# SyncE's order of transfers in a hybrid attention stage: the write of the turned keys ahead of the reads of u, and ahead of the weight loads

## The chip, the core and the metric

The kernel runs on one core of one Trainium2 chip. The metric is the device time of one execution in microseconds (us); lower is better. A core has a matrix engine (TensorE, PE in the profile; its weight loads, PEld, overlap its matmuls), VectorE (DVE), ScalarE (ACT), GpSimd (POOL), and SyncE (SP), which in this kernel issues every DMA. Each engine runs its own list of instructions in order, and the engines wait for each other by semaphores.

## The reference

The input x is 2 x 2048 x 256 in fp32. Four residual layers follow one another; the change lies in the third.

```python
x = x + attn_a(layernorm(x))      # gated scan
x = x + ffn(layernorm(x))         # ternary weights, gelu
x = x + attn_b(layernorm(x))      # the stage of this study, "C" in the kernel
x = x + ffn(layernorm(x))

# attn_b, 16 heads of 64; q, k, v are projections of the layer's input
def step(carry, qkv):
    S_K, C_QV, G = carry
    q_t, k_t, v_t = qkv
    k_C = einsum('bhk,bhkv->bhv', k_t, C_QV)
    G = G + k_t[..., :, None] * k_C[..., None, :]
    S_K = S_K + k_t[..., :, None] * k_t[..., None, :]
    C_QV = C_QV + q_t[..., :, None] * v_t[..., None, :]
    S_C = einsum('bhkj,bhjv->bhkv', S_K, C_QV)
    o_t = einsum('bhk,bhkv->bhv', q_t, S_C - G)
```

## The kernel before

Stage C cuts the sequence into chunks of 128 tokens and works through 32 turns (`UNITS`). Turn j handles one chunk and half of the heads of both batches, in the form of masked score matrices plus a carried state. The order of every engine's work is written out by hand, one loop over j for each engine.

TensorE's list in turn j is: the scores of the queries with the keys (`scores_of`, L1027, into the banks SB), the product with the state (`by_state`, L1039), the second scores of turn j-1 with u as keys (L1027 again), `u_by_scores` of turn j (L1047), `state_change` and `o_by_scores` of turn j-1 (L1064, L1069, L1081), and then what `between(j)` puts there. That last part sets the kind of the turn:

- **projecting turns** (`qk_set(j)`: j % 4 is 3 or 0): the queries and keys of a coming half are projected (`project`, L201 to L203), with the output product of turn j-1 (L1096 to L1098) in the middle;
- **turns without projections**: the values of a coming chunk are projected (`values`, L1013 to L1015), and in one turn of eight (j % 8 is 5) the next block's normalised rows are transposed as well.

Two operands of TensorE are needed in rows instead of columns: the keys (`krow`) and u (`urow`). Both are turned in three steps. DVE transposes 32 x 32 blocks (`turn_keys` L1269 into `k32`, `turn_u` L1276 into the first half of `sc_a`). SyncE writes that tile to DRAM (the **save**, 512 KB, L914) and, once it has landed, reads it back in another order with four DMAs of 128 KB (the **lands**, L917): the keys back into `k32`, u into the second half of `sc_a`. ACT copies the landed tile into `krow` or `urow` (`store_rows`, L1200). TensorE waits for `krow` of turn j before `u_by_scores(j)` (`krow_done`), and for `urow` of turn j-1 before `state_change(j-1)` (`urow_done`).

Some order holds around these copies. ACT copies `urow` of turn j and then `krow` of turn j+1, after the last copy of a projection (the `urow` copy of a projecting turn stands before the last two of them). DVE masks the scores of turn j+1 into `sc_a` (`mask_scores`, L1258) only after `urow` of turn j was copied, since `sc_a` also holds the landed u; the second scores of TensorE need the banks that this mask empties. DVE turns u of turn j, adds two tiles of outputs (L1299), and then turns the keys of turn j+1; in a projecting turn these keys are projected in that very turn. SyncE also loads the projection's weights from DRAM into `ring_hi` and `ring_lo` (`load_weights`, L934; x = 1 are the keys' weights, x = 0 the queries'), four DMAs of 256 KB for each x, as TensorE is done with the weights that lie there.

Of the kernel before, what the change touches and what calls it, by code (L numbers as in the profile page):

```python
# [25 lines left out]
NSUB = T // SUB  # L26
GP = 4
UNITS = NSUB * 4
# [5 lines left out]
def hybrid_kernel(nc, x_d, gamma_d, wqkva_d, wq_d, wk_d, wv_d, wo_d, w1_d, b1_d, w2_d, b2_d, out_d):  # L34
# [13 lines left out]
    with outer:  # L48
        def sbuf(stack, name, shape, dtype=FP32):
            return stack.enter_context(nc.sbuf_tensor(name, shape, dtype))  # L50
# [58 lines left out]
        rows_dram = {x: nc.dram_tensor(f"{x}_rows_scratch", (P, 4, 8 * 32), FP32, kind="Internal").ap() for x in ("k", "u")}  # L109
# [734 lines left out]
        with ExitStack() as st:  # L844
# [7 lines left out]
            k32 = sbuf(st, "k32", [P, 4, 2, 4, 32])  # L852
# [3 lines left out]
            turned = sc_a[:, 0:2, :, :].rearrange("p a m t -> p (a m t)").rearrange("p (t g m d) -> p t g m d", t=4, g=2, m=4)  # L856
            landed = sc_a[:, 2:4, :, :].rearrange("p a m t -> p (a m t)").rearrange("p (r g m d) -> p r g m d", r=4, g=2, m=4)
# [12 lines left out]
            u_turned, u_saved, u_landed, urow_done = sem("C_uturned"), sem("C_usaved"), sem("C_uland"), sem("C_urow")  # L870
            k_turned, k_saved, k_landed, krow_done = sem("C_kturned"), sem("C_ksaved"), sem("C_kland"), sem("C_krow")
# [8 lines left out]
            LAST_STATE = UNITS - 2  # L880
# [10 lines left out]
            def qk_set(j):  # L891

                if j % 4 == 0:
                    return j // 2 + 1 if j < UNITS else None
                return (j + 1) // 2 if j % 4 == 3 and j + 1 < UNITS else None
# [10 lines left out]
            def ring_of(ring, x, pp, pairs=1):  # L906

                return ring[:, :].rearrange("p (n x c) -> p n x c", n=GP, x=2)[:, pp:pp + pairs, x, :]

            @block.sync  # L910
            def _(sp):
                def move(scratch, turned_tile, landed_tile, saved, landing, count):

                    sp.dma_start(scratch, turned_tile.rearrange("p t g m d -> p t (g m d)")).then_inc(saved, 16)  # L914
                    sp.wait_ge(saved, 16 * (count + 1))
                    for t in range(4):
                        sp.dma_start(landed_tile[t * 32:(t + 1) * 32, :, :, :, :].rearrange("p r g m d -> p r (g m d)"),  # L917
                                     scratch.rearrange("(r p) t c -> t p r c", r=4)[t]).then_inc(landing, 16)

                def move_k(j):  # L920
                    sp.wait_ge(k_turned, 2 * (j + 1))
                    move(rows_dram["k"], k32[:, :, :, :, :], k32[:, :, :, :, :], k_saved, k_landed, j)

                def move_u(j):
                    sp.wait_ge(u_turned, 2 * (j + 1))
                    move(rows_dram["u"], turned, landed, u_saved, u_landed, j)

                def load_weights(s, x):

                    for pp in range(0, GP, 2):  # L930
                        sp.wait_ge(qk_ready, 8 * (s - 1) + GP * (1 - x) + pp + 2)
                        pair = slice(s % 2 * GP + pp, s % 2 * GP + pp + 2)
                        for part, ring in ((0, ring_hi), (1, ring_lo)):
                            sp.dma_start(ring_of(ring, x, pp, 2).bitcast(FP32), wqk_dram[part][:, pair, x, :])\  # L934
                                .then_inc(slot_loaded[(1 - x) * 2 + pp // 2], 16)

                move_k(0)
                for x in (1, 0):
                    load_weights(1, x)
                for j in range(UNITS):  # L940
                    if j < LAST_STATE:
                        move_u(j)
                    s = qk_set(j)
                    if s is not None and s + 1 < 2 * NSUB:
                        load_weights(s + 1, 1)
                    if j + 1 < UNITS:
                        move_k(j + 1)
                    if s is not None and s + 1 < 2 * NSUB:
                        load_weights(s + 1, 0)
                    if j == UNITS - 3:  # L950
                        sp.wait_ge(v_ready, 4 * 2 * NSUB)
                        sp.dma_start(wv_hi[:, :, :].rearrange("p a b -> p (a b)").bitcast(FP32), w1t_dram).then_inc(tern_loaded, 16)
                        sp.dma_start(wv_lo[:, :, :].rearrange("p a b -> p (a b)").bitcast(FP32), w2t_dram).then_inc(tern_loaded, 16)
                for x in range(GP):
                    sp.wait_ge(slot_loaded[x], 32 * (2 * NSUB - 1))
                sp.wait_ge(tern_loaded, 32)
                sp.wait_ge(k_landed, 64 * UNITS)
                sp.wait_ge(u_landed, 64 * LAST_STATE)
# [392 lines left out]
```

## Time and profile before

| what | value |
|---|---|
| time, median of 3 runs | 1164.42 us (1162.98 to 1165.89) |
| time of the profiled execution | 1162.61 us |
| its span, first to last instruction | 1160.9 us |
| mean granted TensorE clock over the span | 0.983 of full speed |
| stage C in the trace | from about 280 us to 1025 us of the span |
| TensorE busy | 1090.5 us, 94% of the span |
| VectorE, ScalarE, GpSimd busy | 689.1, 573.8, 212.1 us |
| DMA | 124.20 MB, mean 107 GB/s |

Busy time of an engine that others do not wait for says little. What counts is the time in which TensorE stands idle, what ended that idleness, and the times at which the transfers behind it were issued. Times of rows are microseconds from the span's start. In a row of the timeline the first number is the start, the second how long the instruction or the merged group took, xN the number of instructions, and the bracket the idle time of the engine before it with what ended it.

### The profile page before, as it was taken

How to read it: one execution, taken by the hardware profiler on the slowest of the kernel's cores; microseconds unless marked ns; L12 is line 12 of the kernel's file. 1: busy time of each engine (PE TensorE's matmuls, PEld its weight loads, DVE VectorE, ACT ScalarE, POOL GpSimd, SP SyncE). 2: the span in 40 equal slices, each digit the busy share in tenths (PEclk: the TensorE clock that was granted, in tenths of full speed). 3: DMA queues.
4: the chain of work that ended last, by engine and by line, in shares of the span. 5: the costliest groups of instructions: out<-in, count | busy, mean ns of one | idle time of the engine just before them, and what ended most of it. 6: DMA issues, size and time to landing. Idle time of an engine off the chain costs nothing. (4 is left out here: it accounts for less than half of the span.)

```text
span 1160.9 us, 26806 instructions
## 1 busy us (share of the span) xinstructions
PE 1090.5 (94%) x11150; PEld 974.2 (84%) x11150; DVE 689.1 (59%) x1281; ACT 573.8 (49%) x1001; POOL 212.1 (18%) x177
## 2 busy tenths in 40 slices
PE   5897799998899999999999999999999999779998
PEld 4675588897789998898989899988889888768987
DVE  6999697771353574355475445466445357357783
ACT  4222666662454454445455544555455445246663
POOL 2326262120010101001110110021001010122230
PEclk9998899999999999999999999999999999899999
DMA  9000360003434524543642552453453344101011
GB/s 300 22 1 1 117 212 36 0 1 104 151 107 147 167 93 130 181 128 104 181 155 74 164 180 94 147 164 116 137 168 124 114 128 147 37 2 37 19 36 55
DMA packets 96320, 124.20 MB, mean 107 GB/s; under 512 B 8784, under 2 KB 86480, under 8 KB 95440
## 3 DMA queue, kind: packets, MB, share of 16 engines
q1 hardware_dynamic: 96208, 122.59, 33.0%
q8 instruction: 85, 1.39, 0.5%
q14 instruction: 27, 0.22, 0.1%
HBM read 79.57 MB, written 42.99 MB: 106 GB/s over the span
## 5 line engine op out<-in xcount | busy, mean ns | idle before, releaser
L972 POOL TENSOR_TENSOR ot_lo<-o_sum,ot_hi 128x512 fp32r<-128x512 f32 x64 | 82.3, 1289 | 644.6 <-ACT ot_hi L1194 642.4
L1258 DVE TENSOR_TENSOR sc_a<-bank,causal 128x512 f32<-128x512 f32 x128 | 79.6, 684 | 98.4 <-PE bank L1027 97.5
L1225 ACT COPY ut<-bank 64x512 f32<-64x512 f32 x128 | 74.2, 579 | 66.9 <-PE bank L1047 64.5
L201 PE MATMUL bank<-ln_xhi,ring_hi 128*128 128x512 f32 x256 | 102.4, 400 | 3.8 <-POOL state L962 3.3
L202 PE MATMUL bank<-ln_xlo,ring_hi 128*128 128x512 f32 x256 | 100.6, 393 | 0.0
L203 PE MATMUL bank<-ln_xhi,ring_lo 128*128 128x512 f32 x256 | 100.3, 392 | 0.0
L1258 DVE TENSOR_TENSOR ln_xn<-bank,causal 128x512 f32<-128x512 f32 x128 | 79.5, 684 | 34.3 <-PE bank L1027 34.3
L1200 ACT COPY krow<-k 128x512 f32<-128x512 f32 x64 | 36.4, 616 | 120.5 <-DMA k<-k_rows_scratch 120.5
L1269 DVE STREAM_TRANSPOSE k<-kt 128x512 f32<-128x512 f32 x64 | 43.4, 697 | 72.8 <-ACT kt L1184 72.8
L1320 DVE TENSOR_TENSOR xres<-bank,xres 128x512 f32<-128x512 f32 x32 | 22.0, 689 | 105.7 <-PE bank L1098 105.7
L1096 PE MATMUL bank<-wo_hi,ot_hi 128*128 128x256 f32 x256 | 74.9, 292 | 8.5 <-POOL ot_lo L972 8.5
L815 DVE TENSOR_TENSOR D_hid_lo<-D_hidden,D_hid_hi 128x512 fp32r<-128x512 f32 x64 | 57.5, 921 | 32.1 <-ACT D_hid_hi L764 31.6
L1291 DVE TENSOR_TENSOR state<-bank,state 128x512 f32<-128x512 f32 x60 | 41.5, 692 | 58.2 <-PE bank L1069 58.2
L1229 ACT COPY o_sum<-bank 64x512 f32<-64x512 f32 x128 | 74.2, 579 | 2.4
L1184 ACT COPY qt<-bank 128x512 f32<-128x512 f32 x64 | 37.4, 586 | 75.4 <-PE bank L203 75.4
L815 DVE TENSOR_TENSOR B_hid_lo<-B_hidden,B_hid_hi 128x512 fp32r<-128x512 f32 x64 | 59.6, 954 | 25.3 <-ACT B_hid_hi L764 24.9
L1097 PE MATMUL bank<-wo_lo,ot_hi 128*128 128x256 f32 x256 | 74.2, 290 | 0.0
L1098 PE MATMUL bank<-wo_hi,ot_lo 128*128 128x256 f32 x256 | 74.1, 289 | 0.0
L1047 PE MATMUL bank<-sc_a,krow 128*64 128x128 f32 x1024 | 63.5, 277 | 10.7 <-ACT krow L1200 10.5
L1047 PEld LDWEIGHTS bank<-sc_a,krow 128*64 128x64 f32 x1024 | 55.6, 137 | 15.6 <-ACT krow L1200 13.7
L775 ACT ACTIVATE D_hidden<-bank,b_sb 128x512 f32<-128x512 f32 x64 | 44.2, 692 | 47.7 <-PE bank L713 41.7
L1027 PEld LDWEIGHTS bank<-qt,kt 64*128 64x128 f32 x1024 | 59.7, 188 | 9.0 <-issue 5.3
(124 smaller groups left out, 2992.5 us busy)
## 6 DMA issues: line engine op xcount, KB each, us to landing
k_rows_scratch<-k SPq DMA_DIRECT2D x32, 512.0 KB, 4.0
k<-k_rows_scratch SPq DMA_DIRECT2D x128, 128.0 KB, 2.8
ring_hi<-wqk_hi_scratch SPq DMA_DIRECT2D x60, 256.0 KB, 3.9
ring_lo<-wqk_lo_scratch SPq DMA_DIRECT2D x60, 256.0 KB, 4.9
u_rows_scratch<-sc_a SPq DMA_DIRECT2D x30, 512.0 KB, 2.6
sc_a<-u_rows_scratch SPq DMA_DIRECT2D x120, 128.0 KB, 2.9
out_dram<-xres SPq DMA_DIRECT2D x6, 512.0 KB, 2.9
xres<-in_L_attn_a_x_dram SPq DMA_DIRECT2D x4, 512.0 KB, 7.3
```

The lines of the kernel that those rows point to most:

```text
L201: nc.tensor.matmul(out, w_hi, x_hi, start=(k == 0), stop=False)
L202: nc.tensor.matmul(out, w_hi, x_lo, start=False, stop=False)
L203: return nc.tensor.matmul(out, w_lo, x_hi, start=False, stop=(k == last_k))
L815: nc.vector.tensor_tensor(hid_lo[:, b, f, :], hidden[:, f % 4, :], hid_hi[:, b, f, :].bitcast(FP32), ALU.subtract).then_inc(hlow_done, 1)
L972: nc.gpsimd.tensor_tensor(ot_lo[:, g, :, :].rearrange("p m t -> p (m t)"), o_sum[:, (j - 1) % 2, g, :], ot_hi[:, g, :, :].rearrange("p m t ...
L1047: last = nc.tensor.matmul(bank[CB[2 * g + h]][half(h), m * P:(m + 1) * P], krow[:, j % 2, g, m, half(h)], sc_a[:, 2 * g + h, m, :], start= ...
L1096: nc.tensor.matmul(dst, ot_hi[:, g, m, :], w[0], start=first, stop=False)
L1097: nc.tensor.matmul(dst, ot_hi[:, g, m, :], w[1], start=False, stop=False)
L1098: last = nc.tensor.matmul(dst, ot_lo[:, g, m, :], w[0], start=False, stop=done)
L1225: nc.scalar.copy(ut[half(h), g, :, :].rearrange("p m t -> p (m t)"), bank[CB[x]][half(h), :])\
L1229: nc.scalar.copy(o_sum[half(1 - h), j % 2, g, :], bank[CB[x]][half(1 - h), :]).then_inc(os_done, 1)
L1258: nc.vector.tensor_tensor(to[:, x, :, :], bank[SB[x]][:, :].rearrange("p (m t) -> p m t", m=4), causal[:, None, :].to_broadcast([P, 4, P]) ...
```

## The change

The helper `move` (save, wait for it, four lands) is cut into `save_turned` and `land_rows`, and SyncE's loop gets another order. Nothing else changes: no instruction is added or removed, and the lists of the other engines stay as they are.

```diff
-                move_k(0)
+                save_k(0)
+                land_k(0)
                 for x in (1, 0):
                     load_weights(1, x)
                 for j in range(UNITS):
+                    s = qk_set(j)
                     if j < LAST_STATE:
-                        move_u(j)
-                    s = qk_set(j)
-                    if s is not None and s + 1 < 2 * NSUB:
-                        load_weights(s + 1, 1)
-                    if j + 1 < UNITS:
-                        move_k(j + 1)
-                    if s is not None and s + 1 < 2 * NSUB:
-                        load_weights(s + 1, 0)
+                        save_u(j)
+                    if s is not None:
+                        if j < LAST_STATE:
+                            land_u(j)
+                        save_k(j + 1)
+                        land_k(j + 1)
+                        if s + 1 < 2 * NSUB:
+                            load_weights(s + 1, 1)
+                            load_weights(s + 1, 0)
+                    else:
+                        if j + 1 < UNITS:
+                            save_k(j + 1)
+                        if j < LAST_STATE:
+                            land_u(j)
+                        if j + 1 < UNITS:
+                            land_k(j + 1)
```

```diff
+                def save_turned(scratch, tile, ready, saved, count):
+
+                    sp.wait_ge(ready, 2 * (count + 1))
+                    sp.dma_start(scratch, tile.rearrange("p t g m d -> p t (g m d)")).then_inc(saved, 16)
+
+                def land_rows(scratch, tile, saved, landing, count):
+
+                    sp.wait_ge(saved, 16 * (count + 1))
                     for t in range(4):
```

SyncE's list in a turn without projections (turn 5), before. C_uturned and C_kturned are the semaphores of DVE's transposes, C_usaved and C_ksaved those of the saves.

```order
L914 DMA u_rows_scratch<-sc_a 128x1024 [waits C_uturned]
L917 DMA sc_a<-u_rows_scratch 32x4x256 [waits C_usaved]
L917 DMA sc_a<-u_rows_scratch 32x4x256 x3
L914 DMA k_rows_scratch<-k 128x1024 [waits C_kturned]
L917 DMA k<-k_rows_scratch 32x4x256 [waits C_ksaved]
L917 DMA k<-k_rows_scratch 32x4x256 x3
```

The same turn in the changed kernel, whose line 915 is the save and 921 the lands:

```order
L915 DMA u_rows_scratch<-sc_a 128x1024 [waits C_uturned]
L915 DMA k_rows_scratch<-k 128x1024 [waits C_kturned]
L921 DMA sc_a<-u_rows_scratch 32x4x256 [waits C_usaved]
L921 DMA sc_a<-u_rows_scratch 32x4x256 x3
L921 DMA k<-k_rows_scratch 32x4x256 [waits C_ksaved]
L921 DMA k<-k_rows_scratch 32x4x256 x3
```

The keys' save has moved past the wait for u's save and the four reads of u, and those reads now stand behind the wait for the turned keys.

SyncE's list in a projecting turn (turn 3), before, behind that turn's u. C_qk counts the projected tiles of TensorE.

```order
L934 DMA ring_hi<-wqk_hi_scratch 128x2x256 [waits C_qk]
L934 DMA ring_lo<-wqk_lo_scratch 128x2x256
L934 DMA ring_hi<-wqk_hi_scratch 128x2x256 [waits C_qk]
L934 DMA ring_lo<-wqk_lo_scratch 128x2x256
L914 DMA k_rows_scratch<-k 128x1024 [waits C_kturned]
L917 DMA k<-k_rows_scratch 32x4x256 [waits C_ksaved]
L917 DMA k<-k_rows_scratch 32x4x256 x3
L934 DMA ring_hi<-wqk_hi_scratch 128x2x256 [waits C_qk]
L934 DMA ring_lo<-wqk_lo_scratch 128x2x256
L934 DMA ring_hi<-wqk_hi_scratch 128x2x256 [waits C_qk]
L934 DMA ring_lo<-wqk_lo_scratch 128x2x256
```

The same place in the changed kernel, whose line 942 is the weight load:

```order
L915 DMA k_rows_scratch<-k 128x1024 [waits C_kturned]
L921 DMA k<-k_rows_scratch 32x4x256 [waits C_ksaved]
L921 DMA k<-k_rows_scratch 32x4x256 x3
L942 DMA ring_hi<-wqk_hi_scratch 128x2x256 [waits C_qk]
L942 DMA ring_lo<-wqk_lo_scratch 128x2x256
L942 DMA ring_hi<-wqk_hi_scratch 128x2x256 [waits C_qk]
L942 DMA ring_lo<-wqk_lo_scratch 128x2x256
L942 DMA ring_hi<-wqk_hi_scratch 128x2x256 [waits C_qk]
L942 DMA ring_lo<-wqk_lo_scratch 128x2x256
L942 DMA ring_hi<-wqk_hi_scratch 128x2x256 [waits C_qk]
L942 DMA ring_lo<-wqk_lo_scratch 128x2x256
```

The four loads of the keys' weights have moved behind the whole move of the keys; the four of the queries' weights stand where they stood.

## Rows read from the trace of the kernel before

**Rows 1.** Busy time by stage: us, PE, PEld, DVE, ACT, POOL, PEclk, DMA share, GB/s

```profile
280.00:1002.00 722.00, 705.05 (x8861) 640.67 (x8861) 373.25 (x645) 358.30 (x638) 87.00 (x76) 1.00 0.43 138
```

**Rows 2.** Who waited for whom: us in total, times, longest us

```profile
ACT krow L1200 <- DMA k<-k_rows_scratch: 120.5, 30, 8.2
ACT urow L1200 <- DMA sc_a<-u_rows_scratch: 14.9, 12, 2.6
PE bank L1047 <- ACT krow L1200: 10.5, 12, 4.1
```

**Rows 3.** Timeline of PE at three of these waits

```profile
315.43 0.77 PE L1047 MATMUL bank<-sc_a,krow 128*64 128x128 f32 x10 [4.09 <-ACT krow L1200]
...
540.28 1.42 PE L1047 MATMUL bank<-sc_a,krow 128*64 128x128 f32 x22 [0.47 <-ACT krow L1200]
...
908.00 1.97 PE L1047 MATMUL bank<-sc_a,krow 128*64 128x128 f32 x32 [1.44 <-ACT krow L1200]
```

**Rows 4.** Busy time around the longest wait and around the one at 908

```profile
316.70:320.10 3.40, 3.40 (x60) 3.40 (x58) 0.40 (x1) 3.08 (x6) 0.00 (x0) 0.50 0.07 23
907.00:911.00 4.00, 3.00 (x74) 3.01 (x76) 1.24 (x3) 2.75 (x6) 0.00 (x0) 1.00 0.01 4
```

**Rows 5.** Timeline of SP, turn 10, without projections

```profile
525.94 0.34 SPq L914 DMA_DIRECT2D u_rows_scratch<-sc_a  x1
528.58 1.73 SPq L917 DMA_DIRECT2D sc_a<-u_rows_scratch  x4
530.36 0.43 SPq L914 DMA_DIRECT2D k_rows_scratch<-k  x1
533.87 1.73 SPq L917 DMA_DIRECT2D k<-k_rows_scratch  x4
```

**Rows 6.** Timeline of DVE, same stretch

```profile
527.01 1.28 DVE L1269 STREAM_TRANSPOSE k<-kt 128x512 f32<-128x512 f32 x2
...
535.37 2.48 DVE L1258 TENSOR_TENSOR sc_a<-bank,causal 128x512 f32<-128x512 f32 x4 [0.39 <-PE bank L1027]
```

**Rows 7.** Timeline of ACT, same stretch

```profile
532.79 1.14 ACT L1200 COPY urow<-sc_a 128x512 f32<-128x512 f32 x2 [0.78 <-DMA sc_a<-u_rows_scratch]
539.09 1.14 ACT L1200 COPY krow<-k 128x512 f32<-128x512 f32 x2 [5.16 <-DMA k<-k_rows_scratch]
```

**Rows 8.** Timeline of PE, same stretch

```profile
537.85 1.95 PE L1027 MATMUL bank<-qt,ut 64*128 64x128 f32 x32
```

**Rows 9.** Busy time and DMA, one microsecond of the same stretch

```profile
527.00:528.00 1.00, 1.00 (x6) 0.84 (x5) 1.00 (x3) 0.66 (x2) 0.00 (x0) 1.00 1.00 410
```

**Rows 10.** Timeline of SP, turn 7, a projecting one

```profile
462.51 0.34 SPq L914 DMA_DIRECT2D k_rows_scratch<-k  x1
469.94 1.74 SPq L917 DMA_DIRECT2D k<-k_rows_scratch  x4
...
473.24 0.47 SPq L934 DMA_DIRECT2D ring_lo<-wqk_lo_scratch  x1
```

**Rows 11.** Timeline of ACT, then PE, behind turn 7

```profile
474.23 1.14 ACT L1200 COPY krow<-k 128x512 f32<-128x512 f32 x2 [4.16 <-DMA k<-k_rows_scratch]
...
480.93 0.50 PE L201 MATMUL bank<-ln_xhi,ring_hi 128*128 128x512 f32 x1
```

**Rows 12.** Timeline of SP, turn 0, the first projecting one

```profile
298.82 3.05 SPq L917 DMA_DIRECT2D sc_a<-u_rows_scratch  x4
...
303.93 0.47 SPq L914 DMA_DIRECT2D k_rows_scratch<-k  x1
310.00 1.74 SPq L917 DMA_DIRECT2D k<-k_rows_scratch  x4
```

**Rows 13.** Timeline of DVE, then ACT, behind turn 0

```profile
300.40 0.71 DVE L1269 STREAM_TRANSPOSE k<-kt 128x512 f32<-128x512 f32 x1 [1.50 <-ACT kt L1184]
...
314.24 1.14 ACT L1200 COPY krow<-k 128x512 f32<-128x512 f32 x2 [7.69 <-DMA k<-k_rows_scratch]
```

**Rows 14.** The weight loads' line, from issue to landing, us

```profile
DMA to landing us min/median/max: 3.1/4.3/7.1
```

More of the change, by code:

```diff
@@ L911, in _, with save_k, land_k, save_u @@
             def _(sp):
-                def move(scratch, turned_tile, landed_tile, saved, landing, count):
-                    sp.dma_start(scratch, turned_tile.rearrange("p t g m d -> p t (g m d)")).then_inc(saved, 16)
+                def save_turned(scratch, tile, ready, saved, count):
+                    sp.wait_ge(ready, 2 * (count + 1))
+                    sp.dma_start(scratch, tile.rearrange("p t g m d -> p t (g m d)")).then_inc(saved, 16)
+                def land_rows(scratch, tile, saved, landing, count):
                     sp.wait_ge(saved, 16 * (count + 1))
                     for t in range(4):
-                        sp.dma_start(landed_tile[t * 32:(t + 1) * 32, :, :, :, :].rearrange("p r g m d -> p r (g m d)"),
+                        sp.dma_start(tile[t * 32:(t + 1) * 32, :, :, :, :].rearrange("p r g m d -> p r (g m d)"),
                                      scratch.rearrange("(r p) t c -> t p r c", r=4)[t]).then_inc(landing, 16)
[L920 to L926, printed above, removed]
+                def save_k(j):
+                    save_turned(rows_dram["k"], k32, k_turned, k_saved, j)
+                def land_k(j):
+                    land_rows(rows_dram["k"], k32, k_saved, k_landed, j)
+                def save_u(j):
+                    save_turned(rows_dram["u"], turned, u_turned, u_saved, j)
+                def land_u(j):
+                    land_rows(rows_dram["u"], landed, u_saved, u_landed, j)
                 def load_weights(s, x):
```

## The prediction

> **What bounds the kernel now.** I read the busy times of the stages first, because the change only touches SyncE's list in stage C. There TensorE is busy for 705 of 722 us at the full clock [rows 1], so the whole stage has 17 us to give, and only what TensorE stands idle for counts. The table of waits comes next. ACT waits 120.5 us for the landed keys, but TensorE waits only 10.5 us, in 12 places, for the copy `krow` that ACT makes of them [rows 2]. For `urow` TensorE shows no wait at all; ACT waits 14.9 us for its landing [rows 2]. So the 120.5 us are slack of ACT, and 10.5 us are what a faster move of the keys can take from the path. The timeline of PE shows how they are spread: one wait of 4.09 us at 315.43, and small ones, of which 0.47 and 1.44 are shown; 1.44 is the longest of the small ones [rows 3].
>
> The long wait costs more than itself. Behind it TensorE's granted clock is 0.50, that is 1.2 GHz instead of 2.4, for 3.4 us in which the engine is busy throughout; around the wait of 1.44 us the clock stays at 1.00 [rows 4]. 3.4 us at half speed hold 1.7 us of work, so 1.7 us are lost there.
>
> **The change, part 1: turns without projections** (u's save, keys' save, u's lands, keys' lands). I follow turn 10, in front of the wait of 0.47. Before, SyncE issues u's save at 525.94, u's lands from 528.58 to 530.31, the keys' save at 530.36 and the keys' lands from 533.87 [rows 5]. The keys have been turned since 527.01 + 1.28 = 528.29 [rows 6], so their save stands ready for 2.1 us behind u's lands. In the new order it is issued at 528.3, 2.1 us earlier. How long it then takes is bounded by two rows: 2.6 us as u's save did on an empty queue, and 3.5 us as the keys' save did behind u's lands [rows 5]. The keys' lands are therefore issued between 530.9 and 531.8 (u's lands are all issued by 530.5), 2.1 to 3.0 us earlier than 533.87. From there to ACT's copy I take the same 539.09 - 533.87 = 5.2 us [rows 5, 7]. The copy ends at 538.3 at the latest, and TensorE wants it at 540.28 - 0.47 = 539.8. The gain of at least 2.1 us is more than the 1.44 of the longest wait in such a turn, so these waits go to nothing.
>
> What u pays: SyncE now waits for the turned keys (528.29) and issues their save (0.43 us) ahead of u's lands, so these start at about 528.7 instead of 528.58. The least delay is thus 0.15 us. The most is that no read of u moves until the keys' save has landed, at 530.9 to 531.8: 2.3 to 3.2 us. Nearer is the time of the data alone. The DMA engines ran at 410 GB/s and a busy share of 1.00 over the whole microsecond from 527 to 528, with u's save [rows 9]; 512 KB at that rate are 1.3 us. The save at 525.94 was still moving data at the end of that microsecond, about 2.05 us behind its issue, so the keys' save would occupy the engines until about 528.3 + 2.05 = 530.35. Reads that would otherwise have begun about 1.2 us after their issue lose some 0.6 us, and I take a delay of 0.7 us. It costs nothing as long as this cover holds: `urow` is copied by 532.79 + 1.14 = 533.9 [rows 7], and the next user of that tile, DVE's mask, starts at 535.37 [rows 6], 1.4 us later. Behind the mask the second scores of TensorE start at 537.85 [rows 8]; four masks end at 537.85 too, and the last two are wanted only at about the middle of that group, another 0.95 us. So u can be 2.4 us late before TensorE waits. 15 turns without projections move u, so each microsecond beyond 2.4 would cost up to 15 us.
>
> **Part 2: projecting turns** (keys' move ahead of four weight loads). In turn 7 the keys' save is issued at 462.51 in either order, but before it lies behind 1 MB of weights and needs 469.94 - 462.51 = 7.4 us until the lands can go [rows 10]. Without those loads I take the same 2.6 to 3.5 us; the lands go at 465.1 to 466.0, and with 474.23 - 469.94 = 4.3 us [rows 10, 11] the copy could start at 469.4 to 470.3. It is at least 3.9 us earlier, where TensorE's waits behind such turns (turn 0 left out) are about 0.5 us or less. They vanish.
>
> The weights pay. The keys' weights are issued from 466.9 to 467.8 on instead of before 462.1, the queries' behind them, some 3.9 us in all for eight loads if nothing holds them, so the last is issued by about 472, not later than the 473.24 of before [rows 10]. A load takes 4.3 us in the middle and 7.1 at most from issue to landing [rows 14]. The four of the keys' weights, issued by 470, have landed by 477; the next projection begins at 480.93 [rows 11]. 3.9 us of cover are left in the tightest pair of turns (one projecting turn directly behind another). If the cover were gone, each late microsecond would stand on TensorE 7 times, once in each such pair (turns 3 and 4 to turns 27 and 28).
>
> **Part 3: turn 0.** It holds the 4.09 us. The keys are turned at 300.40 + 0.71 = 301.1 [rows 13]; u's lands keep SyncE until 301.87, and the save then stands behind four weight loads, at 303.93, and its lands at 310.00 [rows 12]. In the new order the save goes at about 301.9. With 3.5 us, since u's lands are ahead of it, the keys' lands go at 305.4, 4.6 us earlier, and the copy ends at 314.24 + 1.14 - 4.6 = 310.8. TensorE is ready at 315.43 - 4.09 = 311.3 [rows 3]. If the save takes 2 us more than that, 1.5 us stay; I put 0.2 us down for it. A wait up to 1.44 leaves the clock at 1.00 [rows 4], so the 1.7 us come back too.
>
> **The sum.** 10.5 (12 waits) + 1.7 (the slow clock) - 0.2 (a rest in turn 1) = 12.0 us. Weights and u cost nothing behind their cover. The profiled execution took 1162.61 us, 1.8 below the median of the runs shown; from it 1150.6, from the median 1152.4 us. I predict for the median.
>
> **The rivals.** (a) *u comes late and eats part of the gain.* For it: u's cover is 1.4 us to the mask and 2.4 to TensorE, while the longest delay bounded above is 3.2, and ACT already waits up to 2.6 us for u's landing [rows 2]. Against it: the engines need only 1.3 us for a save's data [rows 9]. At a delay of 2.8 us, between the two bounds' ends, it costs 0.4 x 15 = 6 us: 1158.4. The Trainium skill ("DMA: Bandwidth & Descriptors", section "Queues, rings and completion order") has each DMA engine take a ring's descriptors in the order in which they were put there, which would set u's reads wholly behind the keys' save, and so speaks against this order. By that rule the delay is the end of the save's data, which is the 0.7 us above and leaves 1152.4; if instead the save's completion had to be waited for, it would be 1158.4 and more. The keys' saves of before, 3.5 us behind u's lands and 7.4 behind the weights, agree with it.
>
> (b) *The keys gain less than their issue.* Their lands now share the engines with the last of u's in 15 turns. If that took back the gain until half of the small waits stay (3.2 of 6.4 us) and 1.5 in turn 1, the gain is 12.2 - 4.7 = 7.5: 1156.9.
>
> (c) *The change does nothing that counts*, because the waits belong to something else that ends in the same moment, such as the masks of DVE: 1163 to 1165. Against it: TensorE's second scores end, and then it stands idle until precisely the copy of `krow` is done (539.09 + 1.14 = 540.23 against 540.28) [rows 3, 7].
>
> (d) *Slower: u's lateness becomes the new bound.* The mechanism is that of (a), and it decides from the point where its price passes the gain plus 3.5 us: 2.4 + (12.0 + 3.5) / 15 = 3.4 us of delay. That is beyond the 3.2 of the worst bound, but a read that takes long by itself would reach it. At 4.0 us it costs 1.6 x 15 = 24 us: 1164.4 - 12 + 24 = 1176.4.
>
> **How the numbers follow.** 0.3% (3.5 us) is about what a measurement of this kernel can tell from no change, so "faster" begins below 1160.9. The forecast (all waits gone, 1150 to 1155) has 0.73; (a) 0.10; (b) 0.09; (c) 0.05; (d) 0.03. The likeliest has the time 1152.4. The range reaches down to 1149.5: the 17 us of idleness [rows 1] hold a little more than the waits for `krow`, say 1.4 us, and the runs spread by 1.5 us around their median. Upwards it takes in most of (b) and the near end of (a), to 1157.0. Faster: the forecast, (b), and most of (a), 0.90; the same: (c) and the rest of (a), 0.07; slower 0.03.
>
> **What would show it.** In the profile of the changed kernel TensorE's wait for `krow` falls from 10.5 us to under 1 us, and the half clock behind turn 0 is gone. ACT's wait for the keys' landing falls by 2 us or more a turn, from 120.5 us to some 40 to 60, and its wait for u's landing rises from 14.9 by some 5 to 10. The keys' save is issued right behind its transpose in every turn. DVE shows waits for `urow` at the mask of under 1 us each, and no second scores of TensorE wait for DVE. TensorE shows no wait for weights. The prediction is wrong if TensorE waits for masks or for `slot_loaded`, if the keys' save takes over 4.5 us in turns without projections, or if the half clock comes back elsewhere in the stage.

## The result, and the profile after

The changed kernel takes 1149.71 us in the median of four runs against 1164.26 for the kernel before. One of the four took 1803.06 us at a mean granted clock of 0.559 and is left out of what follows; the other three are 1147.21, 1147.85 and 1151.57. The ratio is 0.9871, with a 95% interval of 0.9847 to 0.9895: faster by the 0.3% that the forecast took as its mark, and by more than it said. The median of the three is 1147.85 us, 1.65 below the lower end of the range. In the profiled executions the time fell from 1162.61 to 1147.21 us, by 15.4, where 12.0 were forecast.

The waits of the changed kernel, in total us, times, longest us:

```profile
ACT krow L1218 <- DMA k<-k_rows_scratch: 29.0, 20, 7.9
ACT urow L1218 <- DMA sc_a<-u_rows_scratch: 25.6, 12, 3.4
...
DVE sc_a L1276 <- ACT urow L1218: 3.8, 3, 1.7
```

They answer to [rows 2]. ACT's wait for the keys fell from 120.5 us to 29.0, its wait for u rose from 14.9 to 25.6, and TensorE's row for `krow`, 10.5 us before, is gone. DVE's wait for `urow` at the mask, one of 0.9 us before, has grown to 3.8 us in three places.

For the window of [rows 1], with PE, PEld, DVE, ACT, POOL, granted clock, DMA share and GB/s, TensorE is now busy for 709.7 of 722 us, where it was 705 [rows 1]. The window is the same, but the program is ahead by up to 15 us at its end, so the two numbers do not cover quite the same work:

```profile
280.00:1002.00 722.00, 709.72 (x8938) 645.56 (x8938) 377.52 (x651) 360.51 (x643) 89.66 (x78) 1.00 0.44 137
```

Turn 10, the one of [rows 5 to 8], in the timelines of SP, ACT, DVE and PE:

```profile
516.49 0.34 SPq L915 DMA_DIRECT2D u_rows_scratch<-sc_a  x1
518.88 0.34 SPq L915 DMA_DIRECT2D k_rows_scratch<-k  x1
519.26 2.26 SPq L921 DMA_DIRECT2D sc_a<-u_rows_scratch  x4
521.74 1.73 SPq L921 DMA_DIRECT2D k<-k_rows_scratch  x4
...
524.67 1.14 ACT L1218 COPY urow<-sc_a 128x512 f32<-128x512 f32 x2 [2.10 <-DMA sc_a<-u_rows_scratch]
526.87 1.14 ACT L1218 COPY krow<-k 128x512 f32<-128x512 f32 x2 [1.05 <-DMA k<-k_rows_scratch]
...
525.94 2.48 DVE L1276 TENSOR_TENSOR sc_a<-bank,causal 128x512 f32<-128x512 f32 x4 [0.39 <-PE bank L1045]
...
528.42 1.95 PE L1045 MATMUL bank<-qt,ut 64*128 64x128 f32 x32
530.30 0.88 PE L1065 MATMUL bank<-sc_a,krow 128*64 128x128 f32 x12
```

Counted from the issue of u's save, the keys' save now goes at 2.4 us instead of 4.4, their lands at 5.3 instead of 7.9, and the copy `krow` starts at 10.4 instead of 13.2 and is done 2.3 us before TensorE's `u_by_scores` at 530.30, which has no idle time in front of it. The copy `urow` starts at 8.2 instead of 6.9.

Turn 7, projecting, in SP's timeline (compare [rows 10]): the save waits 2.7 us, not 7.4, and the last of the eight weight loads goes at 462.52.

```profile
453.56 0.34 SPq L915 DMA_DIRECT2D k_rows_scratch<-k  x1
456.29 1.73 SPq L921 DMA_DIRECT2D k<-k_rows_scratch  x4
458.06 0.43 SPq L942 DMA_DIRECT2D ring_hi<-wqk_hi_scratch  x1
...
462.52 0.47 SPq L942 DMA_DIRECT2D ring_lo<-wqk_lo_scratch  x1
```

And turn 0 with what follows it, SP, ACT and PE, then the busy times and the clock behind it:

```profile
299.46 0.43 SPq L915 DMA_DIRECT2D k_rows_scratch<-k  x1
303.29 1.73 SPq L921 DMA_DIRECT2D k<-k_rows_scratch  x4
...
307.50 1.14 ACT L1218 COPY krow<-k 128x512 f32<-128x512 f32 x2 [3.28 <-DMA k<-k_rows_scratch]
...
308.94 1.31 PE L1065 MATMUL bank<-sc_a,krow 128*64 128x128 f32 x20
...
308.94:312.40 3.46, 3.46 (x92) 3.46 (x92) 2.21 (x4) 2.26 (x5) 0.00 (x0) 1.00 0.84 264
```

The copy ends 0.3 us before TensorE wants it, the wait of 4.09 us is gone, and the clock behind it stays at 1.00 where [rows 4] had 0.50.

**Where the 15.4 us come from.** I cut each profile at the first `u_by_scores` matmul of turns 0, 30 and 31. In the changed kernel these are

```profile
289.51 0.76 PE L1065 MATMUL bank<-sc_a,krow 128*64 128x128 f32 x9
...
966.88 0.55 PE L1065 MATMUL bank<-sc_a,krow 128*64 128x128 f32 x6
```

and 983.77 for turn 31; before, they start at 291.30, 981.00 and 998.98. So 1.8 us were won ahead of turn 0, where the change touches nothing; 12.3 between turns 0 and 30; 1.1 in turn 30 to 31; and 0.2 behind. The second share is the forecast one. The first and the third are not, and the experiments had to say whether they belong to the change.

### The profile page after: what moved, and what is told of

Same layout as the page of the kernel before. It is cut to its first block and busy times, and to the rows that moved or that the text cites. A ratio compares the mean times of both kernels' runs of the same rounds, so it can differ in the third digit from the quotient of the medians.

```text
span 1145.5 us, 26806 instructions
## 1 busy us (share of the span) xinstructions
PE 1086.3 (95%) x11150; PEld 971.3 (85%) x11150; DVE 688.9 (60%) x1281; ACT 573.2 (50%) x1001; POOL 212.5 (19%) x177
## 5 line engine op out<-in xcount | busy, mean ns | idle before, releaser
L1045 PE MATMUL bank<-qt,kt 64*128 64x128 f32 x1024 | 65.8, 278 | 0.7 <-ACT v_all L1207 0.7
L775 ACT ACTIVATE B_hidden<-bank,b_sb 128x512 f32<-128x512 f32 x64 | 44.2, 692 | 42.9 <-PE bank L713 35.7
L1202 ACT COPY kt<-bank 128x512 f32<-128x512 f32 x64 | 37.5, 588 | 53.6 <-PE bank L203 53.6
```

The lines of the kernel that those rows point to most:

```text
L775: nc.scalar.activation(hidden[:, f % 4, :], bank[HB[f % 2]][:, :], ACT.Gelu, bias=b1_sb[:, f:f + 1]).then_inc(gelu_done, 1)
L1045: last = nc.tensor.matmul(bank[SB[2 * g + h]][:, m * P:(m + 1) * P], keys(g, m, h), qt[half(h), p, b, c, :], start=True, stop=True)
L1202: nc.scalar.copy(to[:, s % 2 * GP + x % GP, :, :, :].rearrange("p b c t -> p (b c t)"), bank[QKB[x]][:, :]).then_inc(qk_done, 1)
```

## The experiments

Each profile is read in the same three cuts. "Core" below is the stretch from turn 0 to turn 30, "start" the first cut, "last turn" the time from turn 30 to turn 31. The ratio is that of the times to the kernel before on the same chip, with its 95% interval.

| kernel | start | core | last turn | wait of TensorE for krow | ratio |
|---|---|---|---|---|---|
| before | 291.3 | 689.7 | 17.98 | 10.5 | 1 |
| before, e1 | 290.7 | 689.1 | 18.36 | 9.5 | 1.0002 [0.9988, 1.0016] |
| before, e10 | 290.8 | 688.7 | 18.39 | 8.9 | 0.9985 [0.9963, 1.0007] |
| changed | 289.5 | 677.4 | 16.89 | none | 0.9871 [0.9847, 0.9895] |
| changed, e2 | 291.0 | 677.1 | 16.87 | none | 0.9911 [0.9892, 0.9931] |
| changed, e9 | 290.9 | 678.1 | 18.36 | none | 0.9871 [0.9846, 0.9897] |
| e3, projecting turns only | 290.3 | 681.2 | 18.36 | 4.5 | 0.9951 [0.9934, 0.9969] |
| e4, other turns only | 291.4 | 685.2 | 16.88 | 5.8 | 0.9956 [0.9939, 0.9974] |
| e5, turn 0 only | 291.5 | 685.1 | 16.87 | 6.9 | 0.9938 [0.9917, 0.9958] |
| e6, all but turn 0 | 288.5 | 681.3 | 18.36 | 3.5 | 0.9944 [0.9927, 0.9961] |
| e7, u's lands last | 292.0 | 722.1 | 16.88 | none | 1.0284 [1.0239, 1.0329] |
| e8, turns 1 and 26 old | 290.4 | 679.2 | 18.00 | 3.0 | 0.9903 [0.9868, 0.9938] |
| e11, weights between | 290.9 | 679.2 | 18.39 | 2.5 | 0.9909 [0.9879, 0.9939] |

### Both kernels again (e1, e2, e9, e10)

No edit. The runs e1 to e4 were made on one chip, e5 to e8 on a second and e9 to e11 on a third.

> The kernel before, unchanged, profiled once more. The changed kernel's profiled execution was 15.4 us shorter; 13.4 us of that lie between the first and the last u_by_scores of stage C, and 1.8 us ahead of stage C, where the change touches nothing. Theory (the half clock falls differently in each execution): this execution again shows the 4.1 us wait for krow in turn 1 and the 3.4 us at clock 0.50 behind it, the same sum of waits of TensorE for krow (10 to 11 us), but its other stretches at clock 0.50, ahead of stage C and behind it, lie at other places or have another length than in the first profile, by 3 us of such time or more; ratio to the kernel before 0.999 to 1.001. Rival (the clock is a fixed property of each kernel, and the change moved it everywhere): the same stretches at the same places as in the first profile, among them the one at 268.8 us and the one at 989 us.

> The changed kernel, unchanged, profiled once more. Theory: what the order of transfers itself gives is 12 to 12.5 us inside stage C, the rest of the 15.4 us is the half clock elsewhere; over five rounds the time is 1164.3 - 12.4 - 0 to 2 = 1150 to 1152 us (ratio 0.988 to 0.990). Rival (a further gain of 2 to 3 us comes with the change each time): 1147.5 to 1149.5 us (ratio 0.9855 to 0.9875), and again a turn 31 shorter by 1.1 us and a stage C that starts 1.8 us earlier than before. Both: TensorE's wait for krow is 0, and turns 1 and 26 come late for urow by about 0.5 and 0.4 us.

> The changed kernel once more, for the size of the change. So far its ratio to the kernel before was 0.9871 [0.9847, 0.9895] in one session and 0.9911 [0.9892, 0.9931] in the next, while the stretch from the first to the last u_by_scores was 13.4 us shorter in both pairs of profiles. Theory (1.1 to 1.5 us of the 13.4 are one stretch of half clock in turn 31, which comes and goes whatever the order: three of the five profiles with the old order in turns without projections had it and two of the five with the new one; 12.0 to 12.3 belong to the order): the stretch is 694 us without that half clock or 695.3 with it, and the ratio 0.989 to 0.990. Rival (the first session was right and the gain is 15 us): 0.987.

> The kernel before once more on the same chip. Theory: 706 to 708.5 us from the first to the last u_by_scores, waits for krow of 9 to 11.5 us in all, the one of turn 1 from 3.5 to 4.7; the start of that stretch differs from the profiles so far, which had it between 288.5 and 292.0 us whatever the order of transfers, with the half clock ahead of it. Ratio 0.999 to 1.001. Rival (the start follows the order of transfers): it is later than in the profile of the changed kernel from this call by 1.5 us or more.

The core is 688.7 to 689.7 us in three profiles of before (mean 689.2) and 677.1 to 678.1 in three of the changed kernel (mean 677.5): 11.6 us less, against 12.0 forecast. The start does not follow the order: 290.7 to 291.3 before, 289.5 to 291.0 after, and 288.5 in e6. Nor does the last turn. It takes 16.9 us or, with a stretch of half clock in it, 18.0 to 18.4. Of the profiles with the old order in turns without projections, before, e1, e3 and e10 have that stretch and e5 has not; of those with the new order e6, e8, e9 and e11 have it and the first profile after, e2, e4 and e7 do not. These rows of busy times show that place for the kernel before and the changed kernel; the granted clock is the number behind those of the five engines:

```profile
989.00:992.40 3.40, 3.40 (x17) 3.34 (x17) 0.00 (x0) 0.00 (x0) 0.91 (x1) 0.51 0.44 165
```

```profile
974.50:978.00 3.50, 3.08 (x23) 2.91 (x24) 0.00 (x0) 0.00 (x0) 1.31 (x2) 1.00 0.39 154
```

In both, TensorE had just stood idle for 2.2 us until GpSimd's `ot_lo`, which the change leaves as it was. So the theory of e1 holds in the main: outside the core the half clock falls differently from execution to execution. The 1.1 us of the last turn were that. The 1.8 us of the start do not belong to the order either, but that the half clock moved them is not shown: ahead of turn 0 the two profiles have 20.5 and 17.1 us of it, yet e6 starts earliest with 20.5, and e5 has 34.1 and starts at 291.5. In two points e1 missed its theory: its waits for `krow` were 9.5 us in all, under the 10 to 11, and the half clock behind turn 0 lasted 6.8 us instead of 3.4. The rivals of e1 and e10, a clock fixed for each kernel or a start that follows the order, fell.

e2 fits neither of its expectations: the time, 1148.63 us, lies in the rival's range, the ratio, 0.9911, above both, because the kernel before took only 1159.39 on that chip. The fall was 10.8 us there, and 13.6 on the chip of e9 (1163.14 to 1149.52). The ratio of e9 met its rival's 0.987 and not the 0.989 to 0.990 of the theory, while its core was 11.1 us shorter than the mean of before, and not 15; with the last turn it comes to 696.4, where the theory had 695.3 with a half clock. So whole times and cores disagree by some microseconds, in both directions. Over all these runs the changed kernel stayed within 1146.96 to 1152.05, the kernel before within 1156.21 to 1168.59. Why the latter spreads more was not tried; that its waits for landings are uneven (8.9 to 10.5 us in all, one of them 3.6 to 4.6) is an argument only.

### The two parts alone (e3, e4)

For e3 the loop body of the changed kernel ("...") stands under a condition, and behind it the old order:

```diff
+                    if s is not None:
...
+                    else:
+                        if j < LAST_STATE:
+                            save_u(j)
+                            land_u(j)
+                        if s is not None and s + 1 < 2 * NSUB:
+                            load_weights(s + 1, 1)
+                        if j + 1 < UNITS:
+                            save_k(j + 1)
+                            land_k(j + 1)
+                        if s is not None and s + 1 < 2 * NSUB:
+                            load_weights(s + 1, 0)
```

For e4 that condition is turned round:

```diff
-                    if s is not None:
+                    if s is None:
```

> The new order in projecting turns alone, the old one in the others. Theory (each wait belongs to the transfer in front of it, and the two parts add up): the 4.1 us of turn 1, the 1.7 us of the slow clock behind it, and the waits behind turns 7, 23 and 27 (0.41, 0.51, 0.40) go, about 7.5 us with what turn 1 gives besides: 1156.8 us (ratio 0.9935), while eight waits for krow of together 5.1 us stay. Rival (a move that is earlier in one turn lets the next fall behind, so that the parts do not add up): the waits behind the other turns grow, and the gain is under 5 us. Second rival (the surplus of 2 to 3 us beyond the sum belongs to this part): 1154 us.

> The new order in turns without projections alone, the old one in the projecting turns. Theory: the waits of turn 1 (4.1 us, with the half clock behind it) and behind turns 7, 23 and 27 stay, the other eight (5.1 us) go, u's lateness costs 0.5 us in turn 1 and 0.4 in turn 26: 1164.3 - 4.5 = 1159.8 us (ratio 0.996). Rival (the surplus belongs to this part): 1157 us. Rival (u's lateness costs more where the weights' loads still stand in front of it): 1162 us or more, with waits of TensorE's second scores for DVE's masks.

The waits of e3 and e4:

```profile
PE bank L1077 <- ACT krow L1230: 4.5, 5, 1.7
```

```profile
PE bank L1077 <- ACT krow L1230: 5.8, 4, 4.6
```

Against the mean core of before, e3 wins 8.0 us and e4 4.0; together 11.9, and the whole change wins 11.6. The parts add up, and each takes the waits that stand behind its own turns, so the theories stand and e3's first rival (a gain under 5 us) falls. The waits left in e3 are five of together 4.5 us, not eight of 5.1. Its 1153.9 us are near the 1154 of the second rival, but the kernel before took only 1159.39 on that chip; the ratios, 0.9951 and 0.9956, have the forecast 0.9935 and 0.996 inside their intervals. The times say 5.5 and 4.3 us (1153.9 and 1155.14 against 1159.39) and cannot tell this closely.

### Turn 0 alone, and all but turn 0 (e5, e6)

The condition of e3, for e5 and then for e6:

```diff
-                    if s is not None:
+                    if j == 0:
```

```diff
-                    if s is not None:
+                    if j > 0:
```

> The new order in turn 0 alone, the old one in all later turns. Theory (turn 0 carries the long wait and the half clock behind it, and nothing else hangs on it): the span from the first to the last u_by_scores is 707.5 in the two profiles of before and 694.1 in the two of the changed kernel; here turn 1 is 4.7 us and turn 2 is 1 to 2 us shorter, and the others keep their waits for krow of together 5 to 6.5 us, so it is 701 to 702; time 6 us under the kernel before (ratio 0.995). Rival (turn 0 sets the pace of later turns, which then wait longer): 704 or more. Rival (the half clock behind turn 0 comes whatever the wait is): turn 2 stays at 21.5 us or more, and the gain is 4.7.

> The new order everywhere but in turn 0. Theory: the wait of 4.1 to 4.6 us in turn 1 and the half clock behind it stay, all other waits for krow are gone: 707.5 - 7 = 700.5 us between the first and the last u_by_scores, ratio 0.994; with the run of turn 0 alone it adds up to the whole change. Rival (the parts overlap or help each other): the two gains differ from 13.4 us together by more than 1.5.

The cores fall by 4.1 and 7.9 us, again 12.0 together. Turn 0 by itself is worth at least a third of the change: in e5 turn 1 takes 19.4 us instead of 24.1. From the first cut to turn 31 it has 701.96, inside the 701 to 702 of the theory, but partly by luck: 1.1 to 1.5 us of the gain are a last turn that happened to be without the half clock. The core alone won less than the 4.7 us of turn 1, because waits for the keys came up where the profile of before has none, the largest in turn 17, with a half clock behind it. Turn 2 was to be 1 to 2 us shorter and took 21.3 us, 0.3 less than before: the half clock was gone, but TensorE waited 1.6 us for `krow`, where it had waited 0.3. In e3 and e8, which also have the new order in turn 0 and the old one in turn 1, it waited 1.3 and 1.4 us, and in all three the keys' save behind turn 1 took 5.3 to 5.7 us instead of 3.6 to 3.7. Turn 2 comes down to 20.2 to 20.6 us only where turn 1 has the new order too.

e6 keeps the 0.994 of its theory, with 699.6 us where 700.5 were expected, and the rival falls: the two gains make 13.4 us together. But it contradicts what its theory had taken as settled. Its wait in turn 1 is 3.52 us, and the clock behind it stays at 1.00:

```profile
312.45 1.97 PE L1077 MATMUL bank<-sc_a,krow 128*64 128x128 f32 x32 [3.52 <-ACT krow L1230]
```

```profile
312.00:315.50 3.50, 3.05 (x76) 3.05 (x78) 0.11 (x1) 2.25 (x5) 0.00 (x0) 1.00 0.51 167
```

while in e5 the clock fell behind the wait of 1.96 us in turn 17:

```profile
679.21 2.15 PE L1077 MATMUL bank<-sc_a,krow 128*64 128x128 f32 x22 [1.96 <-ACT krow L1230]
...
678.00:681.40 3.40, 2.19 (x26) 2.19 (x28) 0.87 (x2) 1.77 (x4) 0.00 (x0) 0.76 0.22 75
681.40:684.80 3.40, 3.40 (x80) 3.40 (x78) 0.77 (x2) 2.81 (x6) 0.00 (x0) 0.74 0.02 5
```

So the length of the wait alone does not decide it.

### How late u may be (e7, e8)

```diff
                         if j + 1 < UNITS:
                             save_k(j + 1)
-                        if j < LAST_STATE:
-                            land_u(j)
                         if j + 1 < UNITS:
                             land_k(j + 1)
+                        if j < LAST_STATE:
+                            land_u(j)
```

> The changed kernel, but in turns without projections u's lands stand behind the keys' lands, which makes u later still. u's copy began 6.9 us behind the issue of its save before the change, 8.1 in the changed kernel, and 9.4 in turns 1 and 26, where TensorE lost 0.5 and 0.4 us. Theory (rival (a) of the prediction: u has a cover, and beyond it each late microsecond is paid in each such turn): the copy begins 11 us behind the save, 4.2 later than before, where the rows of turns 1 and 26 put the end of the cover at 2.1: 11 turns that project values lose 2.1 us each, 23 us, with waits of TensorE's second scores for DVE's masks; ratio 1.011 to the kernel before, slower than it. In the four turns that transpose rows ACT is late anyway and little is lost. Rival (the cover is larger, and turns 1 and 26 lost their half microsecond to something else): within 5 us of the changed kernel.

Slower than the kernel before by 33 us, 1195.86 against 1162.63 (ratio 1.028, forecast 1.011). Turn 10 of that kernel, SP, ACT, DVE and PE:

```profile
532.15 0.34 SPq L915 DMA_DIRECT2D u_rows_scratch<-sc_a  x1
...
538.95 1.85 SPq L921 DMA_DIRECT2D sc_a<-u_rows_scratch  x4
...
543.71 1.14 ACT L1218 COPY urow<-sc_a 128x512 f32<-128x512 f32 x2 [5.50 <-DMA sc_a<-u_rows_scratch]
...
544.95 2.48 DVE L1276 TENSOR_TENSOR sc_a<-bank,causal 128x512 f32<-128x512 f32 x4 [3.76 <-ACT urow L1218]
...
545.78 2.50 PE L1045 MATMUL bank<-qt,ut 64*128 64x128 f32 x22 [1.55 <-DVE sc_a L1276]
```

The copy begins 11.6 us behind u's save, the mask waits 3.76 us for it, and TensorE's second scores wait for the mask and then run at its pace. Where no half clock is mixed in, the price can be read to a tenth of a microsecond:

| kernel, turn that moves u | urow copy behind u's save | the next turn, over 19.62 |
|---|---|---|
| changed, 10 | 8.18 | 0.0 |
| changed, 26 | 9.33 | 0.4 |
| changed, 1 | 9.47 | 0.5 |
| e9, 26 | 9.76 | 0.8 |
| e9, 1 | 9.85 | 0.9 |
| e2, 1 | 9.91 | 1.0 |
| e7, 9 | 11.52 | 2.6 |
| e7, 6 | 11.57 | 2.6 |
| e7, 22 | 12.22 | 3.3 |

Each time the price is the lateness beyond 8.94 us, within 0.1. The kernel before started this copy at 6.85 in turn 10, so u's cover was 2.1 us (2.4 in the forecast), and it uses 1.3 of it now (0.7 in the forecast). The mechanism of rival (a) and (d) is real; the changed order stays 0.8 us short of the edge in turn 10. The size was about half of what came. The 23 us of my expectation were to be lost against the changed kernel, and the core is 44.5 us longer than its mean (722.1 against 677.5). The copy came 0.5 us later than I had worked out, 12.1 to 12.6 in some turns, so that by the rule above the eleven turns lose 33.7 us; turn 29 paid 1.8 us as well; and eight stretches of half clock fell into the stage, where the kernel before has one behind turn 0 and one in the last turn. What is left for these eight is about 10 us.

For e8 the condition of e3 becomes:

```diff
-                    if s is not None:
+                    if j not in (1, 26):
```

> The changed kernel, with the old order in turns 1 and 26 alone, the two in which urow came late enough to hold DVE's masks. Theory (u's lateness cost 0.5 to 1.0 us in turn 2 and 0.2 to 0.4 in turn 27, but the old order brings back the waits for krow there, 0.3 and 1.4 to 1.7): 694.1 - 0.9 + 1.9 = 695 us, no better than the changed kernel, ratio 0.991. Rival (those turns are slow for another reason, such as the clock behind the start of the stage): turn 2 stays at 20.2 us or more.

Turns 2 and 27 wait for the keys again and take 21.1 and 21.3 us, the core is 1.7 us longer than the mean of the changed kernel, so by the core the changed kernel stays the fastest; the ratios (0.9903 against 0.9871 and 0.9911) cannot tell the two apart. The stretch to turn 31 is 697.2 us, not 695; 1.1 of that is a half clock in the last turn. Turn 2 is over the 20.2 us of the rival, but not for the rival's reason: it waits 1.41 us for `krow`, more than the 0.3 that I had put down. What makes turns 1 and 26 slow was not tried, but the traces show what comes with it. Outside e7, in turn 26 of every profile, and in turn 1 wherever u's copy is over 8.5 us behind its save, one 16 KB transfer of the instruction queue (q8 in the profile's list of queues), 1.0 to 2.1 us long, begins 5.5 to 7.0 us behind u's save, while u's reads are under way. In e4, e6 and e11 it begins within 0.3 us of the issue of turn 1's save instead, and there turn 1 is as early as its neighbours (8.1 to 8.2 us). In one turn, 22 of e9, such a transfer began at 6.9 us and u's copy was not late, so whether the transfer is the cause stays open.

### The place of the weights (e11)

```diff
                         save_k(j + 1)
-                        land_k(j + 1)
                         if s + 1 < 2 * NSUB:
                             load_weights(s + 1, 1)
+                        land_k(j + 1)
+                        if s + 1 < 2 * NSUB:
                             load_weights(s + 1, 0)
```

> The changed kernel, but in projecting turns the keys' weights are loaded between the keys' save and their lands, so that only the save has moved ahead of them. Theory (the save waited 7.4 us because 1 MB of weights stood ahead of it; the lands behind the weights lose 2 to 3 us of that again, which the 3.8 us between krow and its use hide everywhere but in turn 1, where 0.3 us were left): turn 1 waits 2 to 3 us for krow, with a half clock behind it in some executions, the other turns do not wait: 696 to 698.5 us from the first to the last u_by_scores, ratio 0.991 to 0.993. Rival (only the save's place matters): as the changed kernel, 694 to 695.3. Rival (the lands lose all that the save had won): waits of 0.4 us behind turns 7, 23 and 27 as well.

Behind turn 0, SP, ACT and PE:

```profile
300.86 0.43 SPq L915 DMA_DIRECT2D k_rows_scratch<-k  x1
...
304.44 1.74 SPq L921 DMA_DIRECT2D k<-k_rows_scratch  x4
...
311.11 1.14 ACT L1219 COPY krow<-k 128x512 f32<-128x512 f32 x2 [5.67 <-DMA k<-k_rows_scratch]
...
312.30 0.88 PE L1066 MATMUL bank<-sc_a,krow 128*64 128x128 f32 x12 [1.93 <-ACT krow L1219]
```

Nearly as the theory had it: the save waits 3.6 us with weights behind it instead of in front, the lands then take 6.7 us to the copy instead of 4.2, and turn 1 waits 1.9 us (2 to 3 expected). The stretch to turn 31, 697.6 us, lies in the forecast 696 to 698.5, but with 1.5 us of half clock in the last turn. One wait of 0.6 us came up in turn 12, which none of the expectations named. Both moves, the save's and the lands', are thus worth making; the lands' one pays almost only in turn 1.

## Why the prediction was right in its mechanism and too small in its size

- **Waits for krow, 10.5 us in 12 places:** right. They are gone in all three profiles of the changed kernel; ACT's wait fell further than forecast (29.0 us, not 40 to 60), since ACT is held by the later u first; its wait for u rose by 10.7 us (5 to 10). In turn 10 the save went 2.0 us earlier in its turn (2.1 forecast), took 2.9 us (2.6 to 3.5), and from the lands to the copy it was 5.1 us (5.2).
- **Turn 0:** right in sum. Turn 1 took 19.4 us instead of 24.1. That is 4.7, not the 4.1 of the wait: TensorE had also waited 0.3 us for a copy of queries that stood behind u's copy, and in this profile it no longer does (that wait comes and goes: 0.7 us in e10, none in e1, 0.2 in e3 with the new order). The keys' save took 3.8 us (3.5 forecast), and the wait that I left standing (0.2 us) is not there.
- **The half clock behind turn 0, 1.7 us:** turns 2 of before took 21.56, 22.56 and 21.45 us, all with such a stretch (6.8 us long in the second), and 20.2 to 20.6 in the changed kernel, of which 0.5 to 1.0 are u's. So the gain exists. But I had taken "3.4 us at half clock" as the price of that wait, and e6 has a wait of 3.52 us without it. Nor does turn 0's order bring the 1.7 us back by itself, as my part 3 had it: in e5 turn 2 is only 0.3 us shorter than in the kernel before, since a wait for `krow` of 1.6 us came up there; the 20.2 to 20.6 us need turn 1's order as well.
- **u's cover and delay:** the delay was 1.3 us instead of 0.7, the cover 2.1 instead of 2.4; in 13 of 15 turns nothing came of it. In turns 1 and 26 it cost 0.5 and 0.4 us (up to 1.0 and 0.8 in other executions), so "costs nothing" was wrong by about 1 us, and the waits of DVE reach 1.7 us (2.1 in e2 and e9) where I had said under 1. The rule of the Trainium skill ("DMA: Bandwidth & Descriptors", section "Queues, rings and completion order") that each engine takes descriptors in ring order agrees in its direction: u's copy came 1.3 us later although SyncE began to issue its lands only 0.1 us later in the turn (2.77 us behind u's save instead of 2.64), and e11's lands took 2.5 us longer behind the weights. Something else went into the 1.3 us that I had not counted: the four issues themselves took 2.26 us instead of 1.73.
- **Weights:** right. TensorE has no wait for them in any profile. The last load of turn 7 was issued at 462.52, and the next projection started at 471.50.
- **The sum, 12.0 us:** the core measured 11.6 in the mean of three profiles each, and 12.3 in the first pair. This step stands for the stretch that the change touches.
- **The step that failed is the last one, "the runs spread by 1.5 us around their median"**, with the lower end of the range, 1149.5 us, built on it. I carried a sum that holds for the core to the median of three runs and put everything outside the core at nothing. It does not stand still: the start moved between 288.5 and 292.0 us, the last turn between 16.9 and 18.4 with the half clock, and whole times of one unchanged program spread over 5 us (changed) and 12 us (before). The runs of the changed kernel had their median at 1147.85; over 14 runs (three, five and six together) the mean is 1149.2, and the medians of the kernel before were 1164.26, 1159.39, 1162.63 and 1163.14. How far the range was missed is partly luck: the first comparison has the highest of these four medians and the lowest of the three of the changed kernel. From my starting value of 1164.42, the ratio of e2 (0.9911) gives 1154.1 us, inside the range, and the 0.9871 of the first comparison and of e9 gives 1149.4, just outside. The likeliest gain in whole time is about 13 us, between the 10.8 and the 16.4 that single comparisons showed. How much of what is left beyond the core's 11.6 is systematic stays open: the profiles, three of each kernel, show none of it.

Rivals (b), (c) and (d) did not happen; (a) did in two turns, at about 1 us.

## What to carry to other kernels

A queue that one engine issues in order deserves the same care as an engine's instruction list: put each store where its data becomes ready, and bulk loads with slack behind it. Before doing so, find the edge of each cover by pushing the other transfer too far once (e7 gave it to 0.1 us), since a cover of 2.1 us that now lends 1.3 has only 0.8 left, and look at the latest turn: here turns 1 and 26 were over the edge. And forecast the stretch that the change touches by the profile, but give the whole time a range as wide as repeated executions of one program, not as wide as three runs happen to be.

## What the runs showed of the hardware that I had not expected

Whether TensorE's clock falls behind a wait is not set by the wait's length. It stayed at 1.00 behind 3.52 us of idleness (e6) and fell behind 4.09 us (before) and behind 1.96 us (e5); behind the same 2.24 us in turn 30 it fell in eight of thirteen profiles and stayed in five. Such a stretch lasts 3.4 us and cost 1.1 to 1.5 us there; behind the wait of turn 1 it lasted 6.8 us in two profiles, e1 (4.63 us of idleness) and e4 (4.61).
